# A transformer layer on one core: the experts' second product in two passes, and the rotary attention's next-row statistics spread over periods

## What is computed

```python
def _L0_attn_ref(x, Wq, Wk, Wv, Wo):        # H, KV, HD = 16, 4, 64
    q = q * cos + _rotate_half(q) * sin     # rotary positions, k alike
    attn = einsum('bhqd,bhkd->bhqk', q, k) / sqrt(HD)
    attn = softmax(attn + slopes * (key position - query position))
    return (attn @ v) @ Wo

def _L0_ffn_ref(src, ...):                  # D_FF = 1024, N_EXPERTS = 4
    x = _layer_norm(src + plain_attention(src), ln1_g, ln1_b)
    expert_idx = remainder(floor(x @ router_w + router_b), 4)
    for e in range(4):
        h = relu(x @ W1[e] + b1[e])
        y = h @ W2[e] + b2[e]
        ff_out = ff_out + where(expert_idx == e, y, 0.0)
    return _layer_norm(x + ff_out, ln2_g, ln2_b)
```

## Time and profile before

| | us |
|---|---|
| median of 3 runs (lowest, highest) | 2129.33 (2126.92, 2134.72) |
| the profiled execution's own time | 2123.84 |
| its span | 2121.7 |
| experts, first product to last `e_r` | 778.7 to 1035.0 |
| rotary attention, first load to the end | 1043.9 to 2121.7 |

### The profile page before, as it was taken

One profiled execution on the slowest core, in us unless ns is written; L12 is line 12 of the kernel. 1 busy time (PEld: TensorE's weight loads), 2 busy tenths in 40 slices (PEclk: granted clock), 3 DMA queues, 4 the chain that ended last, 5 costly groups with the idle time before them and its releaser, 6 DMA issues. The chain is left out here.

```text
span 2121.7 us, 36924 instructions
## 1 busy us (share of the span) xinstructions
PE 1855.8 (87%) x12145; PEld 1123.7 (53%) x12146; DVE 1319.6 (62%) x2902; ACT 916.7 (43%) x1313; POOL 983.5 (46%) x673
## 2 busy tenths in 40 slices
PE   5999999999997039999479999999999999999998
PEld 3454454454443038888445554645546465564654
DVE  3767767767765426666566565765657656566661
ACT  2656656656665114444224334242442524335152
POOL 2413233234244534444335737467373764737454
PEclk9999999999999569999879999999999999999999
DMA  5300000000010535555410010100101001010000
GB/s 174 129 6 6 10 0 10 10 0 10 0 60 40 193 115 183 192 191 196 118 31 2 1 41 1 41 1 10 33 1 41 2 11 32 1 41 1 11 21 11
DMA packets 56176, 104.86 MB, mean 49 GB/s; under 512 B 7238, under 2 KB 46566, under 8 KB 50156
## 3 DMA queue, kind: packets, MB, share of 16 engines
q1 hardware_dynamic: 52972, 94.71, 13.1%
q0 software_dynamic: 3072, 8.39, 1.2%
HBM read 76.35 MB, written 26.74 MB: 49 GB/s over the span
## 5 line engine op out<-in xcount | busy, mean ns | idle before, releaser
L369 POOL TENSOR_TENSOR a_probs<-a_probs 128x1024 f32<-128x1024 f32 x144 | 340.7, 2392 | 321.8 <-PE a_psO L696 321.8
L518 DVE CUSTOM_DVE_ANT_0 a_junk<-a_psM,a_alibi 128x512 bf16<-128x512 f32 x512 | 333.6, 688 | 208.8 <-PE a_psM L656 208.8
L1261 DVE TENSOR_REDUCE f_q_tok<-f_psR 128x1 f32<-128x512 f32 x512 | 323.1, 682 | 132.6 <-PE f_psR L1416 132.0
L452 ACT ACTIVATE a_probs<-a_psS 128x1024 f32<-128x1024 f32 x256 | 249.0, 1024 | 284.7 <-PE a_psS L682 284.6
L1199 ACT ACTIVATE f_probs<-f_psS 128x1024 f32<-128x1024 f32 x256 | 248.4, 1025 | 63.7 <-PE f_psS L1435 63.2
L696 PE MATMUL a_psO<-a_probs,a_v 128*32 128x512 f32 x2048 | 244.0, 597 | 0.0
L1416 PE MATMUL f_psR<-f_kP,f_qM 64*128 64x512 f32 x512 | 159.9, 493 | 25.7 <-DVE f_q_tok L1261 17.8
L656 PE MATMUL a_psM<-a_kH,a_qH 64*128 64x512 f32 x512 | 125.6, 486 | 43.8 <-DVE a_n_tok L518 37.5
L1822 ACT ACTIVATE e_h<-e_psH,w_o 128x256 f32<-128x256 f32 x152 | 63.9, 472 | 172.7 <-PE e_psH L1914 172.7
L1448 PE MATMUL f_psO<-f_probs,f_v 128*32 128x512 f32 x1024 | 136.4, 604 | 0.7 <-ACT f_probs L1199 0.6
L656 PEld LDWEIGHTS a_psM<-a_kH,a_qH 64*128 64x128 f32 x512 | 48.6, 186 | 157.3 <-DVE a_n_tok L518 107.4
(11 more groups left out here) (201 smaller groups left out, 3793.5 us busy)
## 6 DMA issues: line engine op xcount, KB each, us to landing
w_w_high<-w_parts SPq DMA_DIRECT2D x19, 1024.0 KB, 5.3
w_w_low<-w_parts SPq DMA_DIRECT2D x19, 1024.0 KB, 7.5
sorted_x<-f_zeros SPq DMA_DIRECT2D x1, 4864.0 KB, 19.9
e_xs<-sorted_x SPq DMA_DIRECT2D x19, 256.0 KB, 2.7
sorted_z<-e_z SPq DMA_DIRECT2D x19, 256.0 KB, 2.2
f_xn<-in_L_attn_x SPq DMA_DIRECT2D x8, 512.0 KB, 3.6
f_w_raw<-in_L_ffn_W SPq DMA_DIRECT2D x4, 1024.0 KB, 9.2
w_parts<-f_w_high SPq DMA_DIRECT2D x4, 1024.0 KB, 3.9
```

What stands on the lines that cost most here:

```text
L369: nc.gpsimd.tensor_tensor(slots, slots, probs[:, first - GRP:first - GRP + 2, :], ALU.add).then_inc(added.sem, 1)
L452: nc.scalar.activation(probs[:, slots, :], psS[:, 2 * p:2 * p + 2, :], ACT.Exp).then_inc(exp_done.sem, 1)
L518: nc.vector.tensor_tensor_reduce(out=junk[:, a, :], in0=psM[:, a, :], in1=alibi[:, h, :], scale=1.0, scalar=-3.0e38, op0=ALU.add, op1=ALU.max,
L1261: nc.vector.tensor_reduce(q_tok[:, c, h, NEG:NEG + 1], psR[:, ring_bank("max", u), :], AX.X, ALU.max, negate=True).then_inc(max_done.sem, 1)
```

## The change

There are four edits. In the experts PE runs the second product in two passes: first the products with `h_high` of both row blocks, then those with `h_low` of both. Each row block has a bank of its own now (`psY[:, t, 0:D]`), so a tile uses both banks, and PE waits for the `e_r` of the tile just before. The waits for `h_rest` are one for each group. In the rotary attention a `bn_stats` stands in each of (1, 1), (1, 2), (1, 3) and (2, 0), with the wait for the rows ahead of the first; the four `bn_aggr` stay in (2, 1). `var_eps` moves from DVE to POOL, ahead of the power. In `PREPARE`, `("out", 4)` and `("max", 1)` change places.

```diff
+    def row_statistics(self, src, t):
+        self.nc.vector.bn_stats(self.stats[:, t, :], src[:, t, :]).then_inc(self.stats_done.sem, 1)
+
+    def aggregate(self, dve, b):
+        for t in range(self.count):
+            dve.wait_ge(self.stats_done.sem, self.stats_done.at(b, t))
+            dve.sem_inc(self.passed, 1)
+            self.nc.vector.bn_aggr(self.aggr[:, t, :], self.stats[:, t, :]).then_inc(self.aggr_done.sem, 1)
+
+    def raise_aggregate(self, pool, b):
+        pool.wait_ge(self.aggr_done.sem, self.aggr_done.at(b, self.count - 1))
+        pool.sem_inc(self.passed, 1)
+        self.nc.gpsimd.tensor_scalar(self.var_eps[:, :], self.aggr[:, :, 1], EPS, None,
+                                     ALU.add).then_inc(self.var_done.sem, 1)
+        self.raise_variance(pool, b)
...
-                                                 ("q", 1), ("max", 0), ("proj", 11), ("max", 1), ("out", 4),
+                                                 ("q", 1), ("max", 0), ("proj", 11), ("out", 4), ("max", 1),
                                                  ("max", 2), ("q", 2), ("out", 4), ("max", 3), ("out", 4),
...
                         if quad == NORM_AT - 1 and more:
-                            norm.raise_variance(pool, b + 1)
+                            norm.raise_aggregate(pool, b + 1)
...
-                        if (quad, j) == (NORM_AT - 1, 1) and more:
-
-                            dve.wait_ge(x_in.sem, x_in.at(b + 1, 0))
-                            norm.statistics(dve, b + 1, xn)
+                        t = TT * (quad + 1 - NORM_AT) + j + 3
+                        if t in range(TT) and more:
+                            if t == 0:
+                                dve.wait_ge(x_in.sem, x_in.at(b + 1, 0))
+                            norm.row_statistics(xn, t)
+                        elif t == TT and more:
+                            norm.aggregate(dve, b + 1)
...
-                nc.vector.tensor_tensor(r2[:, k, :, :], psY[:, k, :].rearrange("p (c n) -> p c n", c=TC),
+                nc.vector.tensor_tensor(r2[:, k, :, :], psY[:, :, 0:D],
...
-                pe.wait_ge(r2_done.sem, r2_done.at(i, k - 2))
...
-                        if t == 0 and n == 2 * MC:
-                            pe.wait_ge(h_rest.sem, h_rest.at(i, 4 * k + 3))
-                        last = nc.tensor.matmul(psY[:, k, t * D:(t + 1) * D], rows[:, m, t * P:(t + 1) * P],
...
+                pe.wait_ge(r2_done.sem, r2_done.at(i, k - 1))
+                from_high = [(m, h_high, w) for m in range(MC) for w in (w2_high, w2_low)]
+                from_low = [(m, h_low, w2_high) for m in range(MC)]
+                for parts in (from_high, from_low):
+                    for t in range(TC):
+                        for n, (m, rows, w) in enumerate(parts):
+                            if t == 0 and rows is h_high and n % 4 == 0:
+                                pe.wait_ge(h_split.sem, h_split.at(i, 4 * k + n // 4))
+                            if t == 0 and rows is h_low and n % 2 == 0:
+                                pe.wait_ge(h_rest.sem, h_rest.at(i, 4 * k + n // 2))
+                            last = nc.tensor.matmul(psY[:, t, 0:D], rows[:, m, t * P:(t + 1) * P],
```

More of the change, by code:

```diff
@@ L309, in _ @@
             norm.set_power(pool)
-            norm.raise_variance(pool, 0)
+            norm.raise_aggregate(pool, 0)
             nc.gpsimd.memset(n_tok[:, :, :], 0.0).then_inc(cleared, 1)
@@ L585, in _ @@
             dve.wait_ge(x_in.sem, x_in.at(0, 0))
-            norm.statistics(dve, 0, xn)
+            for t in range(TT):
+                norm.row_statistics(xn, t)
+            norm.aggregate(dve, 0)
             norm.apply(dve, 0, xn, xn, xn_done)
@@ L1921, in step @@
                     transpose_tile(i, k + 1)
-                pe.wait_ge(r2_done.sem, r2_done.at(i, k - 2))
[L1923 to L1928, removed]
-                        if t == 0 and n == 2 * MC:
-                            pe.wait_ge(h_rest.sem, h_rest.at(i, 4 * k + 3))
-                        last = nc.tensor.matmul(psY[:, k, t * D:(t + 1) * D], rows[:, m, t * P:(t + 1) * P],
-                                                w[:, bass.ds(e, 1), m * D:(m + 1) * D]
-                                                .rearrange("p e n -> p (e n)"), start=(n == 0), stop=(n == len(parts) - 1))
+                pe.wait_ge(r2_done.sem, r2_done.at(i, k - 1))
[9 more added lines that the diff above has]
+                            last = nc.tensor.matmul(psY[:, t, 0:D], rows[:, m, t * P:(t + 1) * P],
+                                                    w[:, bass.ds(e, 1), m * D:(m + 1) * D]
+                                                    .rearrange("p e n -> p (e n)"), start=(rows is h_high and n == 0),
+                                                    stop=(rows is h_low and n == MC - 1))
                 last.then_inc(y_ps.sem, 1)
```

## The result

| | before | with the change |
|---|---|---|
| median of 4 runs, us | 2129.24 | 2096.90 |
| lowest to highest | 2126.92 to 2134.72 | 2091.62 to 2098.55 |
| the profiled execution, own time (span) | 2123.84 (2121.7) | 2098.55 (2096.8) |

The ratio is 0.9846, with a 95% interval of 0.9832 to 0.9861: faster by 32.3 us. All ratios here are of fast runs; one execution of the kernel before, beside e1 to e4, took 2650 us at a mean granted clock of 0.646 and is left out of them. 37.2 us less and 2092 us had been forecast, with a range of 2080 to 2106. By the two profiled executions alone it is 25.3 us. Most of that difference has nothing to do with the change: the experts' first `e_r` starts at 793.58 us before and at 799.10 after, behind stages whose code is the same.

A forecast was written before the change was run, and what follows sets the result against it. The prediction took PE to bound the experts, its idle time being what can be won. It summed -25.7 (experts), -15.8 (statistics) and +4.3 (exchange) to -37.2 us, from 2129.3 to 2092 us, range 2080 to 2106.

The forecast's parts named there:

- The wait in the experts: Experts: PE's wait for DVE ahead of the first `h_low` product goes whole, 18 x 1.43 = 25.7 us off.
- What is late next: Experts: DVE's idle time ahead of `e_r` falls from 2.83 to 1.4 us a tile; groups ready 0.5 us early.
- Rival 2: Experts: the wait shrinks but stays as DVE and POOL meet differently; 11 us given back, 2103 us; chance 0.12.
- Rival 5: Experts: the lost second buffer makes PE wait for `e_r` and the kernel slower, 2142 us for example; chance 0.01.
- The statistics: Rotary attention: the period shrinks from 8.18 to 5.92 us in 7 batches, 15.8 us off, moved `bn_stats` costing nothing.
- rival 3: Rotary attention: the `bn_stats` are not hidden; gain 9.8 us smaller, 2102 us, or 2115 if held by POOL; chance 0.07.
- Epsilon on POOL: Rotary attention: moving `var_eps` off DVE keeps 7.7 of the statistics' 15.8 us.
- The exchange: PREPARE: "out" ahead of maximum 1 delays DVE's chain by 0.62 us in 7 batches, 4.3 us more.
- the own case: Whole kernel: 37.2 us off, median 2092 us; chance 0.58.
- rivals 1 to 3: The first: in PREPARE the exchange costs nothing or pays, 2081 to 2088 us, chance 0.20; the others are Rival 2 and rival 3.
- rival 4: Experts: the wait is for something else, as a DMA, and stays; 2118 us; chance 0.02.

The follow-up runs named there:

- e1: The changed kernel with the old order in PREPARE (maximum 1 ahead of "out"): 2085.22 us, ratio 0.9798 to the kernel before.
- e4: The kernel before with only the statistics spread and the addition of epsilon on POOL: 2111.63 us, ratio 0.9920.
- e6: e1's kernel with one wait for all four groups of low halves in place of one for each group: 2086.95 us, ratio 0.9788.
- e3: The kernel before with only the experts' edits: 2107.30 us, ratio 0.9897.
- e5: e1's kernel with the addition of epsilon left on DVE behind the four aggregates: 2083.57 us, ratio 0.9787 to the kernel before.
- e10: The changed kernel with two "out" products moved between maxima 1 and 2, one each taken from ahead of maxima 7 and 8: 2089.79 us, ratio 0.9807.
- e9: The changed kernel with two "out" products before maximum 1, four after it, one fewer ahead of each of maxima 7 and 8: 2086.45 us, ratio 0.9788.
- e2: The kernel before with only the exchange in PREPARE: 2145.97 us, ratio 1.0076.
- e11: e1 once more, on the same chip as e9 and e10: 2082.40 us, ratio 0.9782 to the kernel before.
- e7: The changed kernel with two "out" products moved from the last "out" to between maxima 1 and 2: 2094.51 us, ratio 0.9833.
- e8: The changed kernel with two "out" products ahead of maximum 1, four between maxima 1 and 2, two fewer in the last "out": 2086.88 us, ratio 0.9794.

## Why the prediction was right and where it was wrong

- **The wait in the experts, 25.7 us.** Right by place and size: 25.2 between the profiles, 1.39 us a tile against 1.43. e6 shows that it is the order of the products. e3, where it stands alone, gave 22, with 25 inside its interval.
- **What is late next.** Right: 1.41 us idle on DVE (1.40), 0.52 us ahead of the first `h_low` (0.5). Rival 2, another meeting of DVE and POOL, fell: three subtractions take 4.82 us, 4.80 before. Rival 5, the lost second buffer, fell too: nothing waits for `e_r`.
- **The statistics, 15.8 us.** Right: e4 gave 17 by the medians and 14.5 between the profiles (last `e_r` to the end), the period is 5.92, and rival 3 fell. A single `bn_stats` takes 0.42 us and not 0.35, and still fits.
- **Epsilon on POOL.** The side remark that the move keeps 7.7 of these 15.8 us was wrong (e5). It took the 1.7 us that the addition was held at its old time and put it at a new time, where POOL runs another operation that ends sooner. What a held instruction costs depends on when the other engine's operation ends. The Trainium skill's rule (GPSIMD Engine Reference, section 4.1, elementwise on VectorE) gave the better answer here, no gain: e5 and e1 are alike, and the addition takes 0.22 us on POOL against 0.170 unheld on DVE.
- **The exchange, +4.3 us: right in sign and place, too small.** The step that failed is the sentence that sums the exchange as "7 x 0.62 = 4.3 us **more**". The 0.62 us is there (0.58 by e10 against e9). What it left out is what the hole ahead of maximum 2 does: I had forecast it at some 1.7 us (1.66 came) and priced it by the time it delays the next instruction, not by the clock behind it. In 5 of 7 batches the second "out" took about 1.5 us longer, 7.5 us in all. 4.3 + 7.5 = 11.8 us; between the changed kernel and e1 it is 11.7 by the medians, 10.2 by the ratios and 10.5 between the profiles. Here the Trainium skill has the mechanism, on its page TensorE: Matmul & The Clock Gate, section HAM oscillation — how this bites in real kernels: a kernel with recurring idle time on PE keeps falling back to the lower clock and climbing again. The rows agree, with shorter waits than the 3 to 5 us for a DMA in the page's example: 1.66 us was enough in 5 of 7 batches. I had read that the clock was at 1.00 before and took it as given after.
- **The total**, stage by stage in the profiles: -25.2 in the experts, 1070.8 - (2121.68 - 1035.04) = -15.8 for the rotary attention without the exchange (e1), +10.5 for the exchange, together -30.5 us; by the medians -32.3, forecast -37.2. The range held it because it was wide enough on the upper side for rival 2, which did not happen: that the total lies inside it is no merit of the exchange's term.
- **Two slips that change no term.** The earlier trace rows gives the 1.71 us to `var_eps` alone, not to it and the four `bn_aggr`. And the chances of the own case and rivals 1 to 3 add up to 0.97, and to 0.98 with half of rival 4's, not to nearly 0.96.

Open stays why the same hole, 1.66 or 2.1 us, is followed by a fall of the clock in some batches and not in others; no run here changes only that.

## What to carry to other kernels

A product that waits for a late operand can be moved behind independent products of the same tile, if each running sum has a bank of its own; read first, from start to start, how many products the wait is worth. Filling a hole on one engine by moving work ahead of an instruction that another engine's chain needs moves the hole and delays the chain: follow both engines through the list before the exchange. Price an idle time on PE that grows by what the clock does behind it as well, and read the granted clock of each candidate, not of the kernel before alone. Work taken away just ahead of a loop's turn may win nothing: look at a batch outside the loop beside it.

## What the runs showed that was not expected

- The same 2.1 us wait on PE at (2, 2) was followed by a fall to the lower clock in 0 of 7 batches of the kernel before, in 3 of 7 in e2 and in 2 of 7 in e3. A fall lengthens a batch by 1.5 us in the changed kernel and e3 and by up to 2.0 in e2, so edits elsewhere in a program move a kernel by some us through it.
- The stages ahead of the experts, whose code is the same in all thirteen profiles, end between 793.5 and 799.1 us (the first `e_r`). This alone moves a run by 5.6 us, more than the difference between e1, e9 and e11. Most of it goes with the clock too, though what sets the clock there is not shown. The windows from 25 to 75 us, of the kernel before, the changed one and e10 in this order, have a granted clock of 0.90, 0.76 and 0.90, and the first `e_r` is at 793.6, 799.1 and 793.5 us:

```profile
25.00:75.00 50.00, 40.01 (x185) 21.09 (x183) 31.52 (x58) 22.21 (x35) 17.60 (x15) 0.90 0.36 117
25.00:75.00 50.00, 41.91 (x160) 23.18 (x159) 27.54 (x52) 19.91 (x32) 16.54 (x14) 0.76 0.25 83
25.00:75.00 50.00, 40.05 (x183) 21.13 (x181) 31.52 (x58) 22.22 (x35) 17.57 (x15) 0.90 0.37 124
```

- Over a turn of the loop PE needs 3.5 to 4.2 us from maximum 8 to maximum 9, with four "out" products between them or two, and 2.8 or 2.1 where the loop is left (e1, e7, e8). The profile names no releaser for the wait; what it consists of is not shown.
